# A Mamba and mixture-of-experts kernel: more of the scan's inputs turned on TensorE, and GpSimd given part of the elementwise work

## The chip, the cores and the metric

The kernel runs on one core of a Trainium2 chip. The metric is the time of one execution on the device in microseconds (us), the median of several runs. Five engines work side by side, each on its own instruction stream, in order: TensorE (PE; its weight loads are shown as PEld), VectorE (DVE), ScalarE (ACT), GpSimd (POOL) and SyncE (SP, which here only starts DMAs). They meet through semaphores.

## The reference

The input is x, 16 sequences of 256 time steps with 128 features. Three stages follow one another: half a mixture of experts (softmax over 8 experts, the top 2 of them, hidden size 512), a mixer, and the same mixture of experts again, each behind a layernorm and added to its input. In the mixer two Mamba blocks (with the same weights apart from the norm) follow one another, and a linear memory follows the second. What the change touches is the scan inside a Mamba block, with 256 channels d and 16 states s:

```python
def step(h, ins):
    d_t, B_t, C_t, u_t = ins
    dA = jnp.exp(d_t[:, :, None] * A)
    h = h * dA + (d_t * u_t)[:, :, None] * B_t[:, None, :]
    y = jnp.einsum('bds,bs->bd', h, C_t)
    return (h, y)
...
y = ys.transpose(1, 0, 2) + xm * D_ssm
y = y * jax.nn.silu(res)
```

## The kernel before

The 16 sequences form 8 groups of two. A group g passes four slots: slots 0 and 1 are the first Mamba block of its two sequences, slots 2 and 3 the second block. q = 4g + i counts slots, 32 in all. Beside the scans of its own slot every engine also does the preparation of the next slot (the head: norm, input projection, convolution, silu, x projection, softplus, du = delta * xm), the rest of the slot before (the tail: gate, output projection, memory), and pieces of the mixtures of experts of neighbouring groups. What each engine does in each of the four kinds of slot, and in which order, is written out by hand in `ORDER`. An engine never leaves that order.

A slot's 16 states are taken in 8 pairs j = 0 to 7. Tiles have 128 partitions; a pair is 2 states x 2 halves of the channels x 256 steps = 1,024 elements in each partition. For each pair:

- `d` (ScalarE, L973): dA = exp(A * delta), four instructions, into one of four buffers.
- The product du * B is made in one of two ways. In a direct pair (0, 2, 4, 6) TensorE spreads two rows of B over all partitions (`t`, L653; a matmul with a selector), and VectorE multiplies by du (`b`, L1331, into `dbu`). In a turned pair (1, 3, 5, 7) du already lies with time on the partitions (`duT`), so that B is a scalar of each partition: ScalarE multiplies with four instructions (`e`, L989, into `scaled`), and TensorE turns the result back into PSUM with eight transposes (`t`, L660).
- `s` (VectorE): the scan, either one of 1,024 elements from `dbu` (L1344) or two of 512 from PSUM (L1350).
- `k` (TensorE, L671) spreads the two rows of C, and `g` (VectorE, L1363) multiplies the states by them: pair 0 into `acc`, the others into one of three buffers `G`.
- `a` (GpSimd, L1602): a DMA that adds `G` to `acc` in memory. The seven of a slot follow one another, each waiting until the one before has landed.

`gate` (VectorE, L1371 to L1377) then waits for the last of them, adds the two states' halves of `acc`, adds D * xm and multiplies by silu(res).

The sorted mixtures of experts run beside this. VectorE finds each token's place (`fplace`, whose last result is `posi`, L1238), GpSimd scatters eight tiles of tokens with indirect DMAs (`sc0` to `sc7`, L1561), TensorE and ScalarE work through 15 tiles (`p`, and `F`, whose outputs L894 are sent out as `results`), GpSimd gathers eight tiles (`ga0` to `ga7`, L1573) once all of `results` have landed, and VectorE adds them up (`fsum`, L1255). Scatters of one mixture and gathers of another fall in slots 1 and 3, and `fsum` is VectorE's last step there; slots 0 and 2 have neither.

ScalarE needs one function table for exp (`d`, `sp`) and another for silu (`r`, `xm`, and the `F` pieces with a silu); each change of table is a load (L843).

## Time and profile before

| | |
|---|---|
| median of 3 runs | 1685.93 us (1684.01 to 1693.28) |
| the profiled execution, first to last instruction | 1689.5 us |
| VectorE busy | 1379.1 us (82%) |
| TensorE busy | 1330.0 us (79%) |
| ScalarE busy | 1278.8 us (76%) |
| GpSimd busy | 572.0 us (34%) |
| granted TensorE clock, mean | 0.90 |
| start up to the first slot's scans | about 87 us |
| from the last slot's end to the end | about 80 us |

Busy means that an instruction of that engine was under way. The profiled execution has only a span of its own, and no separate time on the device is given with it; its span lies 3.6 us above the median and inside the range of the three runs. The slots take some 1,490 us of it.

### The profile page before, as it was taken

How to read it: one execution, taken by the hardware profiler on the slowest of the kernel's cores; microseconds unless marked ns; L12 is line 12 of the kernel's file. 1: busy time of each engine (PE TensorE's matmuls, PEld its weight loads, DVE VectorE, ACT ScalarE, POOL GpSimd, SP SyncE). 2: the span in 40 equal slices, each digit the busy share in tenths (PEclk: the TensorE clock that was granted, in tenths of full speed). 3: DMA queues.
4: the chain of work that ended last, by engine and by line, in shares of the span. 5: the costliest groups of instructions: out<-in, count | busy, mean ns of one | idle time of the engine just before them, and what ended most of it. 6: DMA issues, size and time to landing. Idle time of an engine off the chain costs nothing. (4 is left out here: it accounts for less than half of the span.)

```text
span 1689.5 us, 29263 instructions
## 1 busy us (share of the span) xinstructions
PE 1330.0 (79%) x8754; PEld 1198.4 (71%) x8754; DVE 1379.1 (82%) x2183; ACT 1278.8 (76%) x2660; POOL 572.0 (34%) x617
## 2 busy tenths in 40 slices
PE   7978568878887787878878787887878787568778
PEld 6867457768777686767767676777867676457668
DVE  3367888989888888989889898989889888988732
ACT  3489657978789787978779698878789698549722
POOL 1211423162423426162423536163332523132210
PEclk9988668988999899998999799998999899778889
DMA  7346446675666767676666767675676765455731
GB/s 233 112 95 136 85 83 149 152 169 126 156 158 139 166 142 180 142 170 134 146 159 142 162 146 165 142 179 125 136 175 141 163 148 114 92 129 126 161 88 45
DMA packets 144662, 236.98 MB, mean 140 GB/s; under 512 B 13696, under 2 KB 79488, under 8 KB 144384
## 3 DMA queue, kind: packets, MB, share of 16 engines
q0 software_dynamic: 39424, 132.15, 40.7%
q1 hardware_dynamic: 105088, 102.97, 20.8%
q8 instruction: 77, 1.26, 0.3%
q14 instruction: 73, 0.60, 0.1%
HBM read 92.46 MB, written 25.17 MB: 70 GB/s over the span
## 5 line engine op out<-in xcount | busy, mean ns | idle before, releaser
L1602 POOL DMA_DIRECT2D acc<-G x224 | 204.2, 911 | 855.8 <-DMA acc<-G 422.1
L973 ACT ACTIVATE dA<-delta,A 128x255 f32<-128x255 f32 x1024 | 425.6, 495 | 6.3 <-DVE hs L1344 5.3
L1350 DVE TENSOR_TENSOR_SCAN hs<-dA,b_r 128x512 f32<-128x512 f32 x256 | 297.9, 1202 | 19.9 <-PE b_r L660 12.6
L1363 DVE TENSOR_TENSOR G<-hs,b_r 128x1024 f32<-128x1024 f32 x224 | 272.4, 1216 | 44.8 <-PE b_r L671 34.9
L1344 DVE TENSOR_TENSOR_SCAN hs<-dA,dbu 128x1024 f32<-128x1024 f32 x128 | 292.8, 2287 | 15.1 <-ACT dA L973 8.8
L535 PE MATMUL b_h<-xsT,wst 128*128 128x128 f32 x1680 | 255.5, 301 | 34.4 <-issue 23.3
L535 PEld LDWEIGHTS b_h<-xsT,wst 128*128 128x128 f32 x1680 | 230.5, 212 | 50.7 <-issue 49.0
L547 PE MATMUL b_out<-w2s,hT 128*128 x1680 | 239.0, 289 | 13.5 <-ACT ys L894 9.6
L843 ACT ACT_TABLE_LOAD x182 | 233.5, 1283 | 4.0 <-PEq L1733 0.7
L547 PEld LDWEIGHTS b_out<-w2s,hT 128*128 128x128 f32 x1680 | 219.9, 203 | 18.4 <-issue 17.0
L660 PE MATMUL b_r<-prm,scaled 128*128 128x128 f32 x1024 | 173.5, 300 | 59.7 <-ACT scaled L989 28.8
L989 ACT ACTIVATE scaled<-duT,dtT 128x256 f32<-128x256 f32 x512 | 217.0, 500 | 1.1 <-PE b_r L660 0.8
L660 PEld LDWEIGHTS b_r<-prm,scaled 128*128 128x128 f32 x1024 | 133.3, 156 | 76.5 <-DVE dbu L1331 33.4
L902 ACT ACTIVATE hT<-b_h 128x512 f32<-128x512 f32 x210 | 121.9, 595 | 84.6 <-PE b_h L535 83.5
L671 PE MATMUL b_r<-bcr,selr 128*128 128x256 f32 x512 | 136.0, 349 | 46.6 <-DVE G L1363 36.1
L1331 DVE TENSOR_TENSOR dbu<-du,b_r 128x1024 f32<-128x1024 f32 x128 | 155.3, 1213 | 6.1 <-PE b_r L653 5.8
L1561 POOL DMA_INDIRECT sorted<-xn,posi x112 | 134.7, 1203 | 63.4 <-DVE posi L1238 33.5
L1573 POOL DMA_INDIRECT yk<-results,posi x112 | 128.8, 1150 | 35.9 <-issue 34.2
L600 PE MATMUL b_w<-uT,inx 128*128 128x256 f32 x512 | 138.8, 408 | 1.2 <-ACT uT L918 0.7
L671 PEld LDWEIGHTS b_r<-bcr,selr 128*128 128x128 f32 x512 | 87.7, 207 | 64.3 <-DVE G L1363 45.2
L600 PEld LDWEIGHTS b_w<-uT,inx 128*128 128x128 f32 x512 | 94.4, 200 | 12.1 <-ACT uT L918 1.2
L653 PE MATMUL b_r<-bcr,selr 128*128 128x256 f32 x256 | 67.7, 350 | 42.5 <-DVE hs L1350 42.5
(176 smaller groups left out, 1974.3 us busy)
## 6 DMA issues: line engine op xcount, KB each, us to landing
acc<-G POOLq DMA_DIRECT2D x224, 512.0 KB, 4.8
wst<-w_dram SPq DMA_DIRECT2D x242, 256.0 KB, 2.9
xsort<-sorted SPq DMA_DIRECT2D x70, 192.0 KB, 5.2
results<-ys SPq DMA_DIRECT2D x70, 192.0 KB, 3.0
xin<-x_dram SPq DMA_DIRECT2D x8, 256.0 KB
sorted<-ys SPq DMA_DIRECT2D x2, 960.0 KB, 7.3
sorted<-xn,posi POOLq DMA_INDIRECT x112
yk<-results,posi POOLq DMA_INDIRECT x112
```

The source lines that it names most:

```text
L535: last = mm(H[r % 2][:, w], wst[k % NW][:, w], xsT[i // CH % 2][:, t:t + P], start=True, stop=True)
L547: last = mm(Y[:, i % CH * D:(i % CH + 1) * D], hT[i % NH][:, c, :], w2s[:, e, c, :], start=c == 0, stop=c == HC - 1)
L600: last = mm(o, inx[:, m, r, ch], uT[:, b, PAD - r:PAD - r + T], start=r == 0, stop=r == PAD)
L660: last = nc.tensor.transpose(R[u % 2][:, h * T + t * P:h * T + (t + 1) * P], scaled[k % 2][:, d, t, h * P:(h + 1) * P], ident)
L671: last = mm(C[:, d * T:(d + 1) * T], selr[:, SELECTED.index(DS + DP * j + d), :], bcr[b][:, :], start=True, stop=True)
L843: nc.scalar.preload_act_table_set(name)
L973: last = do(dA[j % 4][:, d, k, 1:], delta[b][:, k, 1:], ACT.Exp, scale=A[:, k, s:s + 1])
L989: last = do(scaled[n % 2][:, d, t, :], duT[b][:, t, :], ACT.Identity, scale=dtT[b][:, s:s + 1])
L1344: V.tensor_tensor_scan(flat(hs[j % 2]), flat(dA[j % 4]), flat(dbu[n % 2]), 0.0, ALU.mult, ALU.add)\
L1350: V.tensor_tensor_scan(hs[j % 2][:, d, :, :].rearrange("p h t -> p (h t)"), dA[j % 4][:, d, :, :].rearrange("p h t -> p (h t)"), R[u % 2][ ...
L1363: V.tensor_tensor(to[:, :, :, :], hs[j % 2][:, :, :, :], both(C).unsqueeze(2).broadcast_to([P, DP, HALVES, T]), ALU.mult).then_inc(q_G, 1)
L1602: Q.dma_start(acc[b][:, :, :, :].rearrange("p d h t -> p (d h t)"), G[j % NG][:, :, :, :].rearrange("p d h t -> p (d h t)"), accum_op=ALU. ...
```

## The change

Only pair 0 stays direct. Pairs 1 to 7 are all turned. Of these ScalarE makes 1, 3, 5 and 7 as before, and GpSimd makes 2, 4 and 6 (`e4`, `e6`, and `h2`, which makes pair 2 of the next slot ahead of it) with four multiplications of 128x256 each. `scaled` has four buffers in place of two. VectorE loses three of four `b` in a slot and has two scans of 512 in place of one of 1,024 in those pairs.

The sums now form two chains of DMAs: pair 0 and the even pairs in `acc`, pair 1 and the odd ones in a second tile, `odd`. Pair 1 is written there directly, and its DMA gives way to `skip`: GpSimd makes D * xm (two multiplications of 128x256) and a DMA adds it to `odd`. GpSimd then adds the halves of `acc` (`w1`), those of `odd`, and the two results (`w2`), three additions of 128x512. Of the four VectorE instructions in `gate` one is left, the product with silu(res).

The selectors are one column each, read 128 times with step zero, in place of full 128x128 tiles; they come with `prm`, so three loads of 512 KB and three casts in the start go. The order of all engines' work in the four kinds of slot is new.

```diff
-TURNED = (1, 3, 5, 7)
-DIRECT = tuple(j for j in range(NP) if j not in TURNED)
+DIRECT = (0,)
+TURNED = tuple(j for j in range(NP) if j not in DIRECT)
+POOLED = (2, 4, 6)
+NS = 4
+AHEAD = (2,)
 SELECTED = [DP * j + d for j in DIRECT for d in range(DP)] + list(range(DS, 2 * DS))
...
+def made_to(q, j):
+
+    by = POOLED if j in POOLED else [t for t in TURNED if t not in POOLED]
+    return q * len(by) + by.index(j) + 1
+
+
+EVEN = (2, 4, 6)
+ODD = ("skip", 3, 5, 7)
...
 ORDER = {
     "tensor": (
-        "p1 t0 k0 t1 in t2 p2 k1 t3 p1 t4 p1 k2 xp p1 t5 dt p1 t6 k3 p1 t7 m1 k4 t8 p1 dx p2 m2 k5 t9 p2 t10 m3 "
-        "t11 k6 p2 m4 k7 p1",
-        "t0 p1 t1 t2 p2 k0 p1 t3 p2 fturn k1 t4 t5 fgate p3 fcount p2 k2 p3 out t6 k3 p5 t7 turn t8 k4 in k5 t9 "
-        "k6 t10 xp t11 dt k7 dx",
-        "t0 p1 t1 p1 t2 p1 k0 t3 p3 k1 out p1 t4 p1 k2 t5 p1 t6 p1 turn t7 k3 in k4 t8 p1 xp t9 t10 dt k5 p1 t11 "
-        "p3 k6 p1 dx p2 k7",
-        "t0 t1 p3 t2 k0 p2 t3 p2 fturn p2 fgate k1 p1 t4 fcount t5 p2 turng k2 p1 in k3 t6 p4 k4 t7 t8 xp dt k5 "
-        "t9 t10 m1 t11 dx k6 m2 m3 k7 m4",
+        "p1 k0 p1 t0 t1 t2 p1 in t3 p2 t4 k1 xp t5 t6 p2 k2 dt p1 k3 t7 k4 t8 t9 p2 m1 dx t10 p1 k5 t11 t12 "
+        "m2 p2 k6 m3 p3 t13 t14 k7 m4 p2",
+        "t0 p1 t1 k0 p3 t2 t3 fturn p1 t4 fgate k1 p1 t5 t6 fcount k2 p5 k3 out t7 p3 k4 t8 t9 p3 turn k5 in "
+        "t10 t11 xp t12 k6 dt t13 dx k7 t14",
+        "p1 t0 p1 t1 p1 t2 p2 k0 t3 p1 k1 out t4 t5 k2 t6 p2 t7 p1 t8 turn p1 k3 in t9 p1 t10 k4 xp t11 t12 "
+        "dt k5 p3 k6 p1 t13 k7 p1 t14 dx p4",
+        "t0 k0 t1 t2 p2 fturn p3 fgate p1 k1 fcount t3 p1 t4 p1 turng p2 t5 p1 t6 p1 t7 t8 k2 in p1 k3 p2 k4 "
+        "xp dt t9 t10 t11 t12 k5 k6 m1 t13 t14 dx k7 m2 m3 m4",
     ),
     "scalar": (
-        "d0 e1 d1 d2 F0 e3 d3 F1 F2 e5 F3 r xm d4 proj d5 sp F4 F5 e7 F6 oT dx F7 d6 d7 v F8 rT",
-        "F9 e1 d0 d1 F10 F11 F12 e3 F13 d2 F14 F15 fxT d3 F16 F17 d4 F18 F19 d5 d6 F20 F21 e5 ftanh F22 F23 e7 "
-        "F24 turned r xm d7 proj sp dx",
-        "d0 e1 F0 d1 F1 F2 e3 F3 e5 F4 d2 d3 d4 d5 d6 turned d7 e7 F5 F6 r xm F7 proj F8 sp F9 F10 F11 dx",
-        "e1 F12 F13 d0 d1 F14 F15 e3 F16 F17 F18 fxT e5 F19 d2 d3 turned d4 F20 F21 ftanh F22 F23 r xm F24 d5 "
-        "proj e7 sp d6 oT dx v d7 rT",
+        "d0 e1 F0 d1 d2 d3 e3 F1 F2 e5 r xm F3 d4 proj e7 F4 F5 sp F6 d5 oT d6 dx d7 v F7 F8 F9 rT",
+        "e1 F10 F11 d0 F12 d1 F13 F14 d2 d3 fxT e3 d4 F15 F16 F17 F18 F19 e5 F20 ftanh d5 F21 d6 F22 F23 F24 "
+        "turned d7 e7 r xm proj sp dx",
+        "e1 d0 F0 d1 F1 d2 d3 F2 F3 e3 F4 d4 e5 d5 d6 turned d7 F5 e7 r xm F6 F7 F8 proj sp F9 F10 F11 dx",
+        "e1 F12 F13 d0 d1 F14 F15 e3 fxT F16 F17 F18 e5 d2 d3 F19 F20 turned F21 d4 d5 ftanh F22 e7 F23 r xm "
+        "F24 proj d6 sp oT d7 dx v rT",
     ),
     "vector": (
-        "b0 s0 g0 s1 gate g1 b2 s2 g2 s3 low b4 g3 delta s4 g4 s5 b6 mask g5 s6 g6 s7 xb g7",
-        "b0 fstats s0 s1 g0 fnorm b2 s2 flog ftop g1 fplace gate g2 s3 b4 xsum g3 un s4 g4 s5 g5 b6 fweights s6 "
-        "g6 low s7 delta g7 fsum",
-        "b0 s0 s1 g0 gate b2 g1 xsum s2 s3 un g2 b4 lx g3 s4 s5 g4 ln b6 low s6 g5 unx delta g6 s7 g7",
-        "b0 fstats s0 s1 fnorm b2 g0 flog ftop g1 fplace s2 g2 s3 gate g3 b4 s4 fweights g4 s5 low g5 b6 delta s6 "
-        "mask g6 s7 g7 xb fsum",
+        "b0 s0 s1 gate g0 s2 g1 s3 g2 low g3 s4 g4 delta s5 s6 mask g5 g6 s7 xb g7",
+        "fstats b0 s0 fnorm g0 s1 s2 flog ftop g1 fplace s3 g2 gate g3 xsum s4 un g4 s5 g5 s6 fweights low "
+        "delta g6 s7 g7 fsum",
+        "b0 s0 s1 g0 gate g1 s2 xsum s3 un g2 lx g3 s4 ln s5 g4 s6 g5 low unx g6 delta s7 g7",
+        "fstats b0 s0 fnorm g0 s1 flog ftop g1 fplace s2 s3 gate g2 s4 fweights g3 g4 s5 low g5 delta s6 g6 "
+        "s7 mask xb g7 fsum",
     ),
     "gpsimd": (
-        "a1 a2 a3 a4 a5 a6 a7",
-        "froot a1 sc0 sc1 sc2 a2 sc3 sc4 fkeep rms a3 sc5 sc6 sc7 rs a4 ga0 ga1 ga2 ga3 a5 ga4 ga5 ga6 ga7 a6 a7",
-        "a1 rms rs a2 a3 lnx rmsx a4 a5 a6 a7",
-        "froot a1 sc0 sc1 sc2 a2 sc3 sc4 fkeep a3 sc5 sc6 sc7 a4 ga0 ga1 ga2 ga3 a5 ga4 ga5 ga6 ga7 a6 a7",
+        "w1 w2 skip e4 e6 a2 a3 a4 a5 a6 h2 a7",
+        "froot e4 w1 w2 skip e6 sc0 sc1 a2 sc2 sc3 rms sc4 sc5 sc6 a3 a4 ga0 ga1 sc7 ga2 rs ga3 ga4 a5 ga5 "
+        "ga6 fkeep ga7 a6 a7 h2",
+        "e4 w1 w2 skip rms e6 a2 rs lnx a3 rmsx a4 a5 a6 h2 a7",
+        "w1 froot w2 skip e4 sc0 e6 sc1 sc2 sc3 a2 sc4 sc5 sc6 a3 sc7 a4 ga0 ga1 ga2 ga3 a5 ga4 ga5 ga6 ga7 "
+        "fkeep a6 a7 h2",
     ),
 }
...
-        selr = sb("selr", [P, len(SELECTED), P], fp32r)
+        selr = sb("selr", [P, len(SELECTED)], fp32r)
...
+        odd = [sb(f"odd{b}", [P, DP, HALVES, T]) for b in range(SEQ)]
+        xd = sb("xd", [P, HALVES, T])
...
-        scaled = [sb(f"scaled{i}", [P, DP, T // P, DI]) for i in range(2)]
-        dbu = [sb(f"dbu{i}", [P, DP, HALVES, T]) for i in range(2)]
+        scaled = [sb(f"scaled{i}", [P, DP, T // P, DI]) for i in range(NS)]
+        dbu = sb("dbu", [P, DP, HALVES, T])
...
+        def scaled_free(q, j):
+
+            k = TURNED.index(j)
+            before = [(p, t) for p in (q - 1, q) for t in TURNED][:len(TURNED) + k]
+            p, t = [x for x in before if x[1] % NS == j % NS][-1]
+            return p * NU + UNIT_OF["S", DP * t + DP - 1] + 1
+
+        def landed(q, j):
+
+            if j in EVEN:
+                return q_even, 16 * (q * len(EVEN) + EVEN.index(j) + 1)
+            return q_odd, 16 * (q * len(ODD) + ODD.index(j) + 1)
...
+            def selector(row):
+                k = SELECTED.index(row)
+                return selr[:, k:k + 1].broadcast_to([P, P])
...
-                was, m = UNITS[u - 2]
-                p = q if u >= 2 else q - 1
+                all_units = q * NU + u
+                p, w = divmod(all_units - 2, NU)
+                was, m = UNITS[w]
+                into = R[all_units % 2]
                 if was == "B":
-                    wait(pe, q_dbu, p * len(DIRECT) + DIRECT.index(m) + 1)
+                    wait(pe, q_dbu, p + 1)
                 else:
                     wait(pe, q_scan, scans_to(p, m // DP) - (DP - 1 - m % DP))
                 if kind == "B":
-                    if n == DIRECT[0]:
-                        pe.wait_ge(q_bc, q + 1)
+                    pe.wait_ge(q_bc, q + 1)
                     for d in range(DP):
-                        last = mm(R[u % 2][:, d * T:(d + 1) * T], selr[:, SELECTED.index(DP * n + d), :], bcr[b][:, :],
+                        last = mm(into[:, d * T:(d + 1) * T], selector(DP * n + d), bcr[b][:, :],
                                   start=True, stop=True)
                 else:
-                    k, d = TURNED.index(n // DP), n % DP
-                    pe.wait_ge(q_sc, q * len(TURNED) + k + 1)
+                    j, d = n // DP, n % DP
+                    pe.wait_ge(q_made if j in POOLED else q_sc, made_to(q, j))
                     for h in range(HALVES):
                         for t in range(T // P):
-                            last = nc.tensor.transpose(R[u % 2][:, h * T + t * P:h * T + (t + 1) * P],
-                                                       scaled[k % 2][:, d, t, h * P:(h + 1) * P], ident)
+                            last = nc.tensor.transpose(into[:, h * T + t * P:h * T + (t + 1) * P],
+                                                       scaled[j % NS][:, d, t, h * P:(h + 1) * P], ident)
                 last.then_inc(q_B, 1)
...
             def du_turned(g, i):
                 q, b = 4 * g + i, i % 2
                 act.wait_ge(q_dumm, q + 1)
+                wait(act, q_made, (q - 1) * len(POOLED))
                 do(duT[b][:, :, :], W[1][:, :].rearrange("p (j d) -> p j d", d=DI), ACT.Copy).then_inc(q_duT, 1)
 
             def scale(g, i, j):
-                q, b, n = 4 * g + i, i % 2, TURNED.index(j)
+                q, b = 4 * g + i, i % 2
                 act.wait_ge(q_duT, q + 1)
-                p, k = (q, n - 2) if n >= 2 else (q - 1, n - 2 + len(TURNED))
-                wait(act, q_B, p * NU + UNIT_OF["S", DP * TURNED[k] + 1] + 1)
+                wait(act, q_B, scaled_free(q, j))
                 for d in range(DP):
                     for t in range(T // P):
                         s = T + t * DS + DP * j + d
-                        last = do(scaled[n % 2][:, d, t, :], duT[b][:, t, :], ACT.Identity, scale=dtT[b][:, s:s + 1])
+                        last = do(scaled[j % NS][:, d, t, :], duT[b][:, t, :], ACT.Identity,
+                                  scale=dtT[b][:, s:s + 1])
                 last.then_inc(q_sc, 1)
...
-                if j:
-                    last = j - NG if j > NG else max(p for p in range(1, NP) if p % NG == j % NG) - (NP - 1)
-                    wait(dve, q_gs, (q * (NP - 1) + last) * 16)
-                to = G[j % NG] if j else acc[i % 2]
+                if j >= 2:
+                    wait(dve, *(landed(q, j - NG) if j - NG >= 2 else landed(q - 1, j - NG + NP - 2)))
+                to = G[(j - 2) % NG] if j >= 2 else (acc, odd)[j][i % 2]
                 V.tensor_tensor(to[:, :, :, :], hs[j % 2][:, :, :, :],
                                 both(C).unsqueeze(2).broadcast_to([P, DP, HALVES, T]), ALU.mult).then_inc(q_G, 1)
 
             def gate_y(g, i):
                 q, b = 4 * g + i, i % 2
-                dve.wait_ge(q_gs, (q + 1) * (NP - 1) * 16)
+                dve.wait_ge(q_sum, 3 * q + 3)
                 dve.wait_ge(q_res, 2 * q + 2)
                 wait(dve, q_omm, q)
-                V.tensor_tensor(yg[:, :, :], acc[b][:, 0, :, :], acc[b][:, 1, :, :], ALU.add)
-                dve.drain()
-                for k in range(HALVES):
-                    V.scalar_tensor_tensor(out=yg[:, k, :], in0=xm[b][:, k, :], scalar=par("D_ssm")[:, k:k + 1],
-                                           in1=yg[:, k, :], op0=ALU.mult, op1=ALU.add)
-                dve.drain()
-                V.tensor_tensor(yg[:, :, :], yg[:, :, :], sres[b][:, :, :], ALU.mult).then_inc(q_yg, 1)
+                V.tensor_tensor(yg[:, :, :], acc[b][:, 0, :, :], sres[b][:, :, :], ALU.mult).then_inc(q_yg, 1)
...
-                wait(pool, q_gs, (q * (NP - 1) + j - 1) * 16)
-                Q.dma_start(acc[b][:, :, :, :].rearrange("p d h t -> p (d h t)"),
-                            G[j % NG][:, :, :, :].rearrange("p d h t -> p (d h t)"),
-                            accum_op=ALU.add).then_inc(q_gs, 16)
+                if j in EVEN:
+                    wait(pool, *(landed(q, j - 2) if j > 2 else landed(q - 1, 6)))
+                    Q.dma_start(flat(acc[b]), flat(G[(j - 2) % NG]), accum_op=ALU.add).then_inc(q_even, 16)
+                else:
+                    pool.wait_ge(*landed(q, j - 2 if j > 3 else "skip"))
+                    Q.dma_start(flat(odd[b]), flat(G[(j - 2) % NG]), accum_op=ALU.add).then_inc(q_odd, 16)
+
+            def skip(g, i):
+
+                q, b = 4 * g + i, i % 2
+                pool.wait_ge(q_xm, 2 * q + 2)
+                for k in range(HALVES):
+                    Q.tensor_scalar(xd[:, k, :], xm[b][:, k, :], par("D_ssm")[:, k:k + 1], 1.0,
+                                    ALU.mult, ALU.mult).then_inc(p_skip, 1)
+                pool.wait_ge(q_G, q * NP + 2)
+                wait(pool, *landed(q - 1, 7))
+                pool.wait_ge(p_skip, 2 * q + 2)
+                Q.dma_start(odd[b][:, 0, :, :], xd[:, :, :], accum_op=ALU.add).then_inc(q_odd, 16)
+
+            def merge(g, i, k):
+
+                q, b = 4 * g + i, i % 2
+                if k == 1:
+                    pool.wait_ge(*landed(q, 6))
+                    Q.tensor_tensor(acc[b][:, 0, :, :], acc[b][:, 0, :, :], acc[b][:, 1, :, :], ALU.add)\
+                        .then_inc(q_sum, 1)
+                else:
+                    pool.wait_ge(*landed(q, 7))
+                    Q.tensor_tensor(odd[b][:, 0, :, :], odd[b][:, 0, :, :], odd[b][:, 1, :, :], ALU.add)\
+                        .then_inc(q_sum, 1)
+                    pool.wait_ge(q_sum, 3 * q + 2)
+                    Q.tensor_tensor(acc[b][:, 0, :, :], acc[b][:, 0, :, :], odd[b][:, 0, :, :], ALU.add)\
+                        .then_inc(q_sum, 1)
+
+            def scale(g, i, j):
+                q, b = 4 * g + i, i % 2
+                pool.wait_ge(q_dt, q + 1)
+                pool.wait_ge(q_duT, q + 1)
+                wait(pool, q_B, scaled_free(q, j))
+                for d in range(DP):
+                    for t in range(T // P):
+                        s = T + t * DS + DP * j + d
+                        last = Q.tensor_scalar(scaled[j % NS][:, d, t, :], duT[b][:, t, :], dtT[b][:, s:s + 1], 1.0,
+                                               ALU.mult, ALU.mult)
+                last.then_inc(q_made, 1)
...
+                for j in AHEAD:
+                    scale(0, 0, j)
...
+                merge(GROUPS - 1, 3, 1)
                 ffn_root(LAST, one)
+                merge(GROUPS - 1, 3, 2)
```

## Rows read from the trace of the kernel before

**Rows 1.** Windows: us, PE, PEld, DVE, ACT, POOL busy (instructions), clock, DMA share, GB/s.
```profile
85.00:1576.00 1491.00, 1167.10 (x7713) 1048.81 (x7711) 1298.22 (x1920) 1204.20 (x2521) 539.60 (x569) 0.89 0.64 142
...
672.00:712.90 40.90, 34.47 (x240) 30.91 (x237) 39.93 (x43) 37.50 (x76) 5.19 (x6) 0.92 0.64 138
712.90:767.40 54.50, 41.09 (x276) 37.30 (x274) 45.63 (x84) 41.59 (x85) 30.13 (x30) 0.87 0.74 168
767.40:813.80 46.40, 39.67 (x281) 37.16 (x282) 43.98 (x70) 41.58 (x86) 14.50 (x19) 0.93 0.66 146
813.80:863.00 49.20, 40.85 (x276) 36.57 (x276) 39.90 (x70) 38.70 (x87) 26.57 (x24) 0.97 0.67 156
```

**Rows 2.** Waits of VectorE, 85 to 1576 us: us in total, times, longest.
```profile
DVE ob L1255 <- DMA yk<-results,posi: 18.5, 6, 4.0
...
DVE xa L1255 <- DMA yk<-results,posi: 14.9, 7, 3.1
```

**Rows 3.** Timeline of VectorE, one second slot: start us, us, operation.
```profile
899.84 1.22 DVE L1331 TENSOR_TENSOR dbu<-du,b_r 128x1024 f32<-128x1024 f32 x1
...
919.71 0.17 DVE L1238 CAST posi<-posf 128x8 uint32<-128x8 f32 x1
...
940.55 2.29 DVE L1344 TENSOR_TENSOR_SCAN hs<-dA,dbu 128x1024 f32<-128x1024 f32 x1
...
952.64 2.35 DVE L1255 SCALAR_TENSOR_TENSOR xa<-yk,c,xa 128x128 f32<-128x128 f32 x8 [3.10 <-DMA yk<-results,posi]
```

**Rows 4.** Timeline of GpSimd, the same slot.
```profile
940.65 2.95 POOL L1573 DMA_INDIRECT yk<-results,posi  x1 [0.31 <-issue]
...
950.12 0.95 POOL L1573 DMA_INDIRECT yk<-results,posi  x1 [0.30 <-issue]
```

**Rows 5.** Groups of VectorE by line: busy us, mean ns of one, idle before.
```profile
L1350 DVE TENSOR_TENSOR_SCAN hs<-dA,b_r 128x512 f32<-128x512 f32 x256 | 297.9, 1202 | 19.9 <-PE b_r L660 12.6 <-ACT dA L973 7.1
...
L1344 DVE TENSOR_TENSOR_SCAN hs<-dA,dbu 128x1024 f32<-128x1024 f32 x128 | 292.8, 2287 | 15.1 <-ACT dA L973 8.8
...
L1331 DVE TENSOR_TENSOR dbu<-du,b_r 128x1024 f32<-128x1024 f32 x128 | 155.3, 1213 | 6.1 <-PE b_r L653 5.8
...
L1374 DVE SCALAR_TENSOR_TENSOR yg<-xm,prm,yg 128x256 f32<-128x256 f32 x64 | 28.2, 482 | 2.5
...
L1371 DVE TENSOR_TENSOR yg<-acc 128x512 f32<-128x512 f32 x32 | 21.9, 683 | 2.7 <-DMA acc<-G 2.5 <-issue 0.2
```

**Rows 6.** Groups of ScalarE and TensorE by line, the same columns.
```profile
L843 ACT ACT_TABLE_LOAD x182 | 233.5, 1283 | 4.0 <-PEq L1733 0.7
...
L660 PE MATMUL b_r<-prm,scaled 128*128 128x128 f32 x1024 | 173.5, 300 | 59.7 <-ACT scaled L989 28.8 <-DVE dbu L1331 24.5 <-DVE hs L1350 6.2
...
L653 PE MATMUL b_r<-bcr,selr 128*128 128x256 f32 x256 | 67.7, 350 | 42.5 <-DVE hs L1350 42.5
```

**Rows 7.** Groups of GpSimd by line, shapes kept apart, the same columns.
```profile
L1561 POOL DMA_INDIRECT sorted<-xn,posi x112 | 134.7, 1203 | 63.4 <-DVE posi L1238 33.5 <-issue 29.0 <-DMA acc<-G 0.9
...
L1573 POOL DMA_INDIRECT yk<-results,posi x112 | 128.8, 1150 | 35.9 <-issue 34.2 <-DMA results<-ys 1.6
...
L1611 POOL TENSOR_TENSOR rs<-xam,x 128x256 f32<-128x256 f32 x16 | 14.6, 910 | 0.2
...
L1579 POOL TENSOR_SCALAR xam<-xa 128x256 f32<-128x256 f32 x2 | 0.8, 400 | 0.0
```

**Rows 8.** One line's instructions: ns min/median/max, first and last start.
```profile
L1561 POOL DMA_INDIRECT sorted<-xn,posi x112: 954/982/2863, 53.5 to 1507.0; - x112
...
L1573 POOL DMA_INDIRECT yk<-results,posi x112: 940/992/2952, 172.8 to 1608.7; - x112
```

**Rows 9.** DMA issues on the page: KB each, median us to landing.
```profile
acc<-G POOLq DMA_DIRECT2D x224, 512.0 KB, 4.8
...
results<-ys SPq DMA_DIRECT2D x70, 192.0 KB, 3.0
```

**Rows 10.** Timeline of ScalarE, the same slot: the last results copied out.
```profile
931.83 0.47 ACT L894 ACTIVATE ys<-b_out 128x384 f32<-128x384 f32 x1
```

74 lines of the change are left out of this document (39 added, 35 removed).

## The prediction

> **What bounds the kernel now.** I read the windows of each kind of slot first. Over all slots VectorE is busy 1,298 of 1,491 us, ScalarE 1,204, TensorE 1,167, GpSimd 540 [rows 1]. The four windows below that row are slots 0 to 3 of one group, cut at each slot's first `g`. In slot 0 VectorE works 39.9 of 40.9 us and in slot 2 44.0 of 46.4: there it is the bound. In slots 1 and 3 it works 45.6 of 54.5 and 39.9 of 49.2, and something else sets the length [rows 1].
>
> VectorE's waits say what: `fsum` waits 18.5 + 14.9 us for gathers, thirteen times [rows 2]. The timelines of one slot 1 show the chain. The slot starts at 899.84, the places are written at 919.88, the last gather's issue ends at 951.07, `fsum` starts at 952.64 after a wait of 3.10 and ends at 954.99 [rows 3, 4]. So 55.2 us = 20.0 (VectorE up to the places) + 31.2 (GpSimd) + 1.6 (landing) + 2.4 (`fsum`). GpSimd's 31.2 us are one unbroken queue by the written order: eight scatters, eight gathers, four accumulating DMAs and three small steps. A GpSimd busy only a third of the time is the bound of half the slots.
>
> **VectorE, removed.** Three `b` at 155.3/128 = 1.21 us each are 3.64 us a slot. A pair turned instead of direct costs two scans of 297.9/256 = 1.16 against one of 292.8/128 = 2.29: 0.04 more, 0.12 a slot. The gate loses one addition (0.68) and two instructions of 28.2/64 = 0.44: 1.57 [rows 5]; their drains I count at nothing. Sum: 3.64 - 0.12 + 1.57 = 5.1 us a slot, 163 us in 32. That is the most the change can give through VectorE. The selectors' casts lie beside a start in which TensorE runs without gaps: nothing.
>
> **TensorE.** 24 more transposes at 173.5/1024 = 0.17 are 4.1 us a slot, six fewer matmuls at 67.7/256 = 0.26 are 1.6 [rows 6]: 2.5 us more. In slot 2 that makes 39.7 + 2.5 = 42.2 of 46.4, part of it at a clock below full (0.93) [rows 1]. It hides behind ScalarE; without that cover it costs up to 2.5 us a slot. The selector weights read with step zero have no row. Between no change and a doubling of their share of the load, 18 loads a slot at the order of 0.1 us, lies 0 to 2 us, hidden too; I take 0.
>
> **ScalarE.** It makes as many products as before. But if I follow the new order through the slots and count where exp and silu alternate, there are 30 more table loads than the 182: two more in each slot 2 and slot 3 that has pieces. 30 x 1.283 = 38.5 us [rows 6]. ScalarE is busy 37.5 of 40.9 in slot 0 and 41.6 of 46.4 in slot 2 [rows 1]; with two loads the latter becomes 44.2. So in slots 0 and 2 it is next in line right behind VectorE. VectorE offers 5.1, ScalarE lets some 2.4 and 2.2 through. It runs up to four pairs ahead and can lend work to slots 1 and 3, where it has room: I take 2.5 for each.
>
> **GpSimd, added.** The multiplication with a column of scalars is in no row. The nearest is the multiplication by a constant on 128x256 at 400 ns [rows 7]. Lower end: that. Upper end: the addition with two tensor inputs of the same size, 910 ns [rows 7]. A column adds one element to each partition's reads, so I take 400: 14 of them are 5.6 us. For the additions of 128x512 there are 910 ns for half the size and twice that; I take 1.3: 3.9 us. Together 9.5 us a slot, 7 to 18 by the ends. The number of DMAs stays at seven.
>
> By the Trainium skill (GPSIMD Engine Reference, Performance versus the Vector engine) an addition of two fp32 tensors costs about 2.6 cycles an element and one-input work runs about at line rate; as an estimate from that page three additions would be 3.3 us instead of 3.9. Its section on engine selection speaks against moving such work to GpSimd at all.
>
> Where does it lie? `e4`, `w1`, `w2`, `skip` and in slot 1 `e6` come ahead of the first scatter, in time that GpSimd now waits away. In slot 3 `e6` (1.6) is inside the chain and `fkeep` has gone out of it. In slots 1 and 3 `h2` comes after the last gather. In slots 0 and 2 the queue has room (5.2 of 40.9 and 14.5 of 46.4 busy [rows 1]). So it is nearly hidden as long as the multiplications cost what I think.
>
> **The new waits.** `w2` waits for pair 7's DMA (4.8 us [rows 9]), and then two additions stand between it and the gate, where VectorE's drop in: 2.6 us later than before. In slots 0 and 2, which follow on late gathers, the gate at 6 to 7 us into the slot is close to that; queued behind it is all of VectorE. I take 0, because ScalarE bounds those slots; the upper end is 3 us. `skip` waits for pair 1's `g`; behind it are `e4` or `e6` and the scatters, and the placing on VectorE takes about as long as they do.
>
> **The gather chain.** Two things shorten it. First, one `b` less ahead of the places: 1.2 us. Second, a gather that started at 940.65, inside a VectorE scan with two inputs in SBUF (940.55, 2.29 us), took 2.95 us [rows 3, 4]; the median is 0.99 [rows 8]. Mean less median over both kinds is (1.203 - 0.982 + 1.150 - 0.992) x 112 = 42 us, 3.0 for each of 14 slots [rows 7, 8]. After the change only pair 0's scan reads `dbu`, ahead of the scatters. I take 2.
>
> The Trainium skill (SBUF — State Buffer, Who interferes with whom) says that a VectorE instruction with two SBUF inputs and a GpSimd instruction that reads SBUF exclude each other for the whole instruction. The trace agrees: 2.95 against 0.99 us.
>
> One thing holds it back: the gathers need the last `results`. They are copied out at 931.83 [rows 10] and land 3.0 us after their issue [rows 9], near 936; gathering began soon after. In slot 3's new order `F24` comes after 32 us of ScalarE's own work where it came after 26 (my count with its durations). There the first gather will wait for it. I take 3 us for slot 1 and 2 for slot 3.
>
> **Sum.** A group gains 2.5 + 3 + 2.5 + 2 = 10 us. Groups 1 to 6: 60. In groups 0 and 7 four slots have little or no expert work, and there VectorE's relief comes through nearly whole, 4 us each, and 2.5 in the other four: 26. The end: the last DMAs no longer form one chain ahead of GpSimd's root: 2. Together 88. 1689.5 - 88 = 1601.5, and as the profiled span stood 3.6 above the median, 1598.
>
> **Rivals.**
> - *VectorE's relief lands whole.* If ScalarE can shift its work and the gather chain shrinks by 5 a slot: 1689.5 - 163 - 3.6 = 1523. For it: ScalarE waits much in slots 1 and 3. Against: 31 us of GpSimd queue.
> - *ScalarE and the chain hold.* The first gather waits for `results` in both slots, the gate for `w2`: slots 1 and 3 stay at 55, groups gain 5: 30 + 18 + 2 = 50, 1636. For it: gathering began only some 2 us after the results; 30 more table loads.
> - *Slower: the multiplication by a column is dear.* If one costs c us, slot 3 has eight of them around the chain and slot 1 four that its slack of some 1 us doesn't hold: a group loses 12(c - 0.4) - 2. From c = 1.4 the gain of 10 is gone; at c = 2 a group is 7 us longer, 6 x 7 = 42, 1728. For it: no such row, and 910 ns with two inputs. Against: 400 ns [rows 7].
> - *No change: the two engines block each other.* GpSimd has 17 more instructions that read SBUF in each slot. If each held VectorE up for 0.3 us, 5.1 are gone, 1680. For it: 2.95 against 0.99, seen from the other side. Against: what VectorE runs is mostly scans and `g` with one input in PSUM; rows 8's medians show that those leave GpSimd alone.
>
> **Numbers.** Forecast 0.50, relief whole 0.14, chain holds 0.20, dear multiplication 0.09, blocking 0.07. About 0.5% (8 us) is what a measurement of this kernel can tell from no change. So faster 0.84, same 0.07, slower 0.09. The likeliest case alone spans 1565 to 1630. The range takes in half of the full relief and most of the chain case, 1545 to 1665, and leaves out about 2 in 10.
>
> **What would show it.** VectorE busy near 1,216 in all; ScalarE near 1,317; 212 table loads; GpSimd near 875. Slots 0 and 2 near 38 and 42 with ScalarE full; slots 1 and 3 near 52, `fsum` still waiting for gathers; indirect DMAs at means near 1.0; multiplications on GpSimd at 0.4. It is wrong if these cost 1 us or more, if VectorE waits at the gate for `w2`, or if the gathers wait for `results` longer than the scatter queue's own length.

## The result, and the profile of the changed kernel

The changed kernel takes 1820.1 us (median of 4 runs, 1808.0 to 1824.4), the kernel before 1685.0 beside it (4 runs). The ratio is 1.078, 95% interval 1.074 to 1.082: slower by 7.8%. The forecast was 1598 us, range 1545 to 1665. Profiled: a span of 1806.2 us against 1689.5.

The head of the page of the changed kernel: busy time, share of the span, instructions of each engine.

```profile
span 1806.2 us, 31047 instructions
...
PE 1422.3 (79%) x9330; PEld 1275.1 (71%) x9330; DVE 1311.7 (73%) x2085; ACT 1327.7 (74%) x2690; POOL 896.1 (50%) x1161
```

VectorE is busy 67 us less than before (1379.1), where 163 us were to go. ScalarE (forecast 1317) and GpSimd (forecast 875) came out near the forecast.

The cuts of [rows 1] at each slot's first `g` don't compare the two kernels: the new order moves a scan and the gate past that `g`. So I cut at pair 0's product `dbu`, the first VectorE work of a slot in both. Slots 0 to 3 of one group, first the kernel before, then the changed one, columns as in [rows 1]:

```profile
859.30:899.80 40.50, 32.12 (x217) 28.77 (x218) 36.86 (x34) 32.90 (x67) 5.16 (x6) 0.92 0.63 140
899.80:954.90 55.10, 40.98 (x291) 36.20 (x290) 46.81 (x92) 44.69 (x91) 29.94 (x30) 0.92 0.73 166
954.90:999.10 44.20, 38.16 (x241) 35.60 (x242) 40.70 (x57) 36.16 (x75) 12.50 (x16) 0.82 0.57 121
999.10:1054.80 55.70, 44.98 (x322) 40.34 (x321) 45.36 (x85) 46.39 (x104) 28.83 (x27) 1.00 0.73 168
```
```profile
923.10:965.00 41.90, 37.62 (x268) 34.71 (x269) 33.90 (x40) 35.55 (x73) 16.90 (x23) 0.92 0.56 125
965.00:1025.70 60.70, 46.35 (x303) 41.91 (x301) 44.00 (x81) 45.19 (x88) 39.37 (x49) 0.86 0.59 141
1025.70:1067.30 41.60, 36.59 (x258) 32.46 (x257) 38.98 (x62) 38.12 (x77) 22.70 (x34) 0.96 0.59 130
1067.30:1130.80 63.50, 46.62 (x316) 41.27 (x315) 46.07 (x74) 47.32 (x101) 37.94 (x44) 0.92 0.59 143
```

Slots 0 and 2 together stayed within 2 us (84.7 and 83.5 here, 81.2 and 83.0 in the mean of groups 1 to 5 below); slots 1 and 3, which carry the scatters and gathers, grew from 55 to 61 and 64 us. VectorE does 44.0 and 46.1 us of work in them, hardly less than before, although three products and most of the gate have gone. Its groups by line say why; the columns are those of [rows 5].

```profile
L1378 DVE TENSOR_TENSOR_SCAN hs<-dA,b_r 128x512 f32<-128x512 f32 x448 | 526.6, 1207 | 185.2 <-PE b_r L691 154.5 <-issue 19.5 <-ACT dA L1005 9.1
...
L1372 DVE TENSOR_TENSOR_SCAN hs<-dA,dbu 128x1024 f32<-128x1024 f32 x32 | 87.7, 2741 | 4.2
...
L1285 DVE SCALAR_TENSOR_TENSOR ob<-yk,c,ob 128x128 f32<-128x128 f32 x56 | 37.8, 734 | 0.5
L1285 DVE SCALAR_TENSOR_TENSOR xa<-yk,c,xa 128x128 f32<-128x128 f32 x56 | 36.1, 704 | 0.7
...
L1185 DVE TENSOR_SCALAR xn<-xin,mv,rstd 128x128 f32<-128x128 f32 x32 | 19.7, 679 | 3.1 <-POOL rstd L1561 3.1
L1185 DVE TENSOR_SCALAR xn<-xb,mv,rstd 128x128 f32<-128x128 f32 x32 | 13.9, 496 | 1.1 <-POOL rstd L1561 1.1
```

The same groups in the kernel before, `fsum` and `xn`:

```profile
L1255 DVE SCALAR_TENSOR_TENSOR xa<-yk,c,xa 128x128 f32<-128x128 f32 x56 | 16.0, 348 | 15.4 <-DMA yk<-results,posi 14.9
...
L1155 DVE TENSOR_SCALAR xn<-xin,mv,rstd 128x128 f32<-128x128 f32 x32 | 8.9, 343 | 7.2 <-POOL rstd L1540 7.2
```

The scan whose second input lies in PSUM costs what it did, 1207 ns against 1202 [rows 5]. The scan with both inputs in SBUF went from 2287 to 2741 ns. `fsum` (L1285; it writes `xa` in slots 1 and `ob` in slots 3) took 348 ns an instruction before in both kinds of slot, and `xn` 343 and 346. The same lines compared over all of VectorE, mean times count, cost some 80 us more: 42 in `fsum`, 15.6 in `xn`, 14.5 in pair 0's scan, the rest small. The first row shows the other change: scans wait 154.5 us for TensorE's turns, against 12.6 [rows 5].

One of the two longest of the fourteen `fsum`s and what GpSimd does beside it, from the two timelines of the changed kernel (VectorE, then GpSimd):

```profile
1229.46 9.81 DVE L1285 SCALAR_TENSOR_TENSOR xa<-yk,c,xa 128x128 f32<-128x128 f32 x8
1239.19 1.21 DVE L1360 TENSOR_TENSOR dbu<-du,b_r 128x1024 f32<-128x1024 f32 x1
```
```profile
1230.46 3.90 POOL L1667 TENSOR_SCALAR scaled<-duT,dtT 128x256 f32<-128x256 f32 x8
1234.25 1.34 POOL L1649 TENSOR_TENSOR acc<-acc 128x512 f32<-128x512 f32 x1
1235.48 1.33 POOL L1653 TENSOR_TENSOR odd<-odd 128x512 f32<-128x512 f32 x1
1236.89 1.26 POOL L1656 TENSOR_TENSOR acc<-acc,odd 128x512 f32<-128x512 f32 x1
1238.14 1.00 POOL L1637 TENSOR_SCALAR xd<-xm,prm 128x256 f32<-128x256 f32 x2
```

Eight instructions that take 2.35 us alone [rows 3] take 9.81, and end 0.1 us after GpSimd's unbroken series of products (`h2` and the next slot's `e4`) and the next slot's sums. GpSimd runs at its own pace meanwhile. One of the eight, 6168 ns long, stands still while most of the products and two additions go by. That `dbu`, with one input in PSUM, costs 1.21 as ever.

Not every `fsum` fares like this. In eight of the fourteen one instruction stands still, for 3.2 us in six of them and for 6.2 us in two. In five the eight instructions take 3.4 us, none over 0.67 us, while GpSimd's products keep their pace of 0.48 us from start to start; the two engines then seem to take turns. The hold-up falls on the next slot's scan instead, which took 5.0 to 5.1 us in four of these five and 3.8 us in the fifth:

```profile
818.16 3.40 DVE L1285 SCALAR_TENSOR_TENSOR xa<-yk,c,xa 128x128 f32<-128x128 f32 x8
821.48 1.21 DVE L1360 TENSOR_TENSOR dbu<-du,b_r 128x1024 f32<-128x1024 f32 x1
822.82 5.00 DVE L1372 TENSOR_TENSOR_SCAN hs<-dA,dbu 128x1024 f32<-128x1024 f32 x1
```

GpSimd's groups in the changed kernel, the columns of [rows 7]:

```profile
L1667 POOL TENSOR_SCALAR scaled<-duT,dtT 128x256 f32<-128x256 f32 x384 | 209.7, 721 | 14.6 <-issue 14.2
L1582 POOL DMA_INDIRECT sorted<-xn,posi x112 | 113.8, 1016 | 46.3 <-issue 28.4 <-DVE posi L1268 17.9
L1594 POOL DMA_INDIRECT yk<-results,posi x112 | 113.1, 1010 | 91.7 <-DMA results<-ys 62.8 <-issue 28.6 <-DMA odd<-G 0.3
...
L1656 POOL TENSOR_TENSOR acc<-acc,odd 128x512 f32<-128x512 f32 x32 | 54.0, 1686 | 2.5
```

The product with a column costs 0.55 us busy, 0.48 from start to start in the series above (its mean of 721 ns counts overlap); scatters and gathers are no longer held up (1203 and 1150 before [rows 7]); but the first gather waits 62.8 us for results, against 1.6. The DMA list of the page has their landing at 4.9 us, against 3.0 [rows 9]:

```profile
results<-ys SPq DMA_DIRECT2D x70, 192.0 KB, 4.9
```

The two medians don't compare like with like: the trace of the changed kernel has the landing of only 42 of the 70 transfers, and in `fsum_clear` below, with all 70, the median is 3.1 us although the first gather waits as long (64.2 us in all). What did grow is the landing of the last results of a slot 1: 3.8 us in the mean of groups 1 to 5 before, 6.0 after.

To see where in a slot the time goes I took milestones from the timelines: us from the slot's `dbu` of pair 0, mean of groups 1 to 5; the last `ys` and the last gather by their ends, the first gather by its start (`all_write_only`, an experiment below, is the changed kernel without GpSimd's new reads).

```
                     slot 1                          slot 3
                 before  changed  all_write_only  before  changed  all_write_only
last ys copied    33.4    34.3      31.1           31.9    34.9      32.1
first gather      38.5    41.3      38.0           38.8    39.7      37.0
last gather       51.3    55.0      51.8           51.3    50.9      48.3
fsum starts       52.9    57.3      54.3           53.2    56.6      53.5
fsum ends         55.3    63.3      56.6           55.5    62.3      55.9
next slot         55.2    63.2      56.5           55.5    62.2      56.3
slots 0 and 2:    before 38.6, 42.6   changed 41.3, 41.7   all_write_only 39.5, 41.0
```

The end of `fsum` is the end of the slot in every column. Of the 14.7 us that slots 1 and 3 grew by, 7.0 are `fsum` itself (2.4 to 6.0 us in slot 1, 2.3 to 5.7 in slot 3), the rest its later start.

### The profile page after: what moved, and what is told of

The parts are those of the page before. It is cut to its first block and busy times, and to the rows that moved or that the text cites. A ratio compares the mean times of both kernels' runs of the same rounds, so it can differ in the third digit from the quotient of the medians.

```text
span 1806.2 us, 31047 instructions
## 1 busy us (share of the span) xinstructions
PE 1422.3 (79%) x9330; PEld 1275.1 (71%) x9330; DVE 1311.7 (73%) x2085; ACT 1327.7 (74%) x2690; POOL 896.1 (50%) x1161
## 5 line engine op out<-in xcount | busy, mean ns | idle before, releaser
L1378 DVE TENSOR_TENSOR_SCAN hs<-dA,b_r 128x512 f32<-128x512 f32 x448 | 526.6, 1207 | 185.2 <-PE b_r L691 154.5
L691 PE MATMUL b_r<-prm,scaled 128*128 128x128 f32 x1792 | 304.3, 304 | 120.3 <-DVE hs L1378 56.8
L691 PEld LDWEIGHTS b_r<-prm,scaled 128*128 128x128 f32 x1792 | 234.1, 157 | 161.6 <-DVE hs L1378 79.7
L874 ACT ACT_TABLE_LOAD x212 | 272.0, 1283 | 4.5 <-PEq L1812 0.7
L1390 DVE TENSOR_TENSOR G<-hs,b_r 128x1024 f32<-128x1024 f32 x192 | 233.2, 1214 | 49.1 <-PE b_r L702 41.7
L1667 POOL TENSOR_SCALAR scaled<-duT,dtT 128x256 f32<-128x256 f32 x384 | 209.7, 721 | 14.6 <-issue 14.2
L702 PE MATMUL b_r<-bcr,selr 128*128 128x256 f32 x512 | 135.7, 349 | 63.7 <-DVE G L1390 59.9
L1630 POOL DMA_DIRECT2D odd<-G x96 | 88.0, 917 | 181.9 <-DVE G L1390 177.0
L1627 POOL DMA_DIRECT2D acc<-G x96 | 90.5, 943 | 157.3 <-DVE G L1390 116.8
L1594 POOL DMA_INDIRECT yk<-results,posi x112 | 113.1, 1010 | 91.7 <-DMA results<-ys 62.8
L702 PEld LDWEIGHTS b_r<-bcr,selr 128*128 128x128 f32 x512 | 86.2, 209 | 80.3 <-DVE G L1390 60.0
L1582 POOL DMA_INDIRECT sorted<-xn,posi x112 | 113.8, 1016 | 46.3 <-issue 28.4
L1642 POOL DMA_DIRECT2D odd<-xd x32 | 29.0, 907 | 198.1 <-DVE odd L1390 130.7
```

Source lines behind the costliest of these rows:

```text
L691: last = nc.tensor.transpose(into[:, h * T + t * P:h * T + (t + 1) * P], scaled[j % NS][:, d, t, h * P:(h + 1) * P], ident)
L702: last = mm(C[:, d * T:(d + 1) * T], selector(DS + DP * j + d), bcr[b][:, :], start=True, stop=True)
L874: nc.scalar.preload_act_table_set(name)
L1378: V.tensor_tensor_scan(hs[j % 2][:, d, :, :].rearrange("p h t -> p (h t)"), dA[j % 4][:, d, :, :].rearrange("p h t -> p (h t)"), R[u % 2][ ...
L1390: V.tensor_tensor(to[:, :, :, :], hs[j % 2][:, :, :, :], both(C).unsqueeze(2).broadcast_to([P, DP, HALVES, T]), ALU.mult).then_inc(q_G, 1)
L1667: last = Q.tensor_scalar(scaled[j % NS][:, d, t, :], duT[b][:, t, :], dtT[b][:, s:s + 1], 1.0, ALU.mult, ALU.mult)
```

## The experiments

All ratios are to the kernel before, run beside each version on the same chip. Its medians there lie between 1684.8 and 1689.6 us, so differences of times taken beside different ones carry up to 5 us. Two theories at the start: **the lock**, GpSimd instructions that read SBUF hold up VectorE instructions with their operands in SBUF; and **the queue**, every scan's input now waits for its turn on TensorE, which has two banks for them.

**1. Reads of GpSimd taken away.** Three kernels write what they would compute.

```
-  Q.tensor_scalar(scaled[...], duT[...], dtT[...], 1.0, mult, mult)      # mult_write_only
+  Q.memset(scaled[...], 0.01)
-  Q.tensor_tensor(acc[b][:, 0], acc[b][:, 0], acc[b][:, 1], ALU.add)     # adds_write_only: the 3 additions
+  Q.memset(acc[b][:, 0], 0.01)                                           # all_write_only: both, and xd
```

> The changed kernel with GpSimd's twelve multiplications of a slot turned into memsets of the same tiles: they write but read nothing, so the products of pairs 2, 4 and 6 are left out of the result. Theory of the lock (GpSimd's reads hold up VectorE's instructions with two inputs in SBUF; the same lines cost VectorE 81 us more than before): fsum's instructions fall from 720 to about 350 ns, pair 0's scan from 2741 to 2290, and the time falls by 50 to 80 us, to 1740 to 1770. Theory of the queue (VectorE waits 154 us for turned units behind other work on TensorE, and the slots 1 and 3 follow a chain of preparation): those durations fall, but the waits grow instead, and the time stays within 20 us of 1820.

> As the one before, and also the three additions and the two multiplications by D of each slot as memsets, so the sums are left out as well: none of the change's work on GpSimd reads SBUF, its DMAs and waits all stay. Lock: another 10 to 20 us less than the kernel with only the multiplications as memsets. Queue: no further change beyond 5 us. If this kernel still stands above 1685, the lock and GpSimd's added time together are not the whole of the loss, and the rest lies in the turned pairs and the order.

> The changed kernel with GpSimd's three additions a slot replaced by writes of the same tiles (the sums over pairs are left out); its twelve products with a column stay. Taking the products' reads away as well brought 1714.6 us from 1782.3. The theory of the lock, with the two kinds of work independent: 1820 - 68 = 1752 us, 1740 to 1765, fsum still near 700 ns (the products stand beside it), scan0 near 2400 and xn near 346 ns. The rival (the additions matter only as time in GpSimd's queue ahead of the products): 1800 us or more, since a write takes nearly as long as an addition.

Measured: `mult_write_only` 1782.3 us (1.054, 1.049 to 1.059), `adds_write_only` 1745.5 (1.034, 1.029 to 1.039), `all_write_only` 1714.6 (1.017, 1.013 to 1.020). Against 1820 taking away the products is worth 38 us, the additions 75, all together 105: nearly the sum. The first is less than the 50 to 80 us expected, and the last gained 68 us over the first where 10 to 20 were expected. In `all_write_only` VectorE's lines are back:

```profile
L1372 DVE TENSOR_TENSOR_SCAN hs<-dA,dbu 128x1024 f32<-128x1024 f32 x32 | 73.4, 2292 | 4.2
...
L1285 DVE SCALAR_TENSOR_TENSOR ob<-yk,c,ob 128x128 f32<-128x128 f32 x56 | 16.0, 346 | 0.6
```

`xn` isn't quite back in this run (460 and 365 ns).

VectorE's busy time fell by 24, 45 and 81 us, in the order of the results. But GpSimd's queue got shorter as well, and its busy time fell by 95, 87 and 210 us. The products' writes in `mult_write_only`:

```profile
L1667 POOL MEMSET scaled<- 128x256 f32 x384 | 117.5, 538 | 13.7 <-issue 13.7
```

That is 0.31 us busy for a write where the product has 0.55; the mean of 538 ns counts overlap. The additions' writes take 0.53 to 0.69 us for 1.4 to 1.7. So these three runs show what GpSimd's new work costs with its reads, 105 of the 135 us, and can't tell the hold-up of VectorE from the longer queue. Experiment 2 can. Some 30 us over the kernel before stay, with 149 us less VectorE work. Two windows of `all_write_only`, a slot 0 and a slot 2, cut at `dbu`, show who ends them now:

```profile
681.20:720.30 39.10, 35.78 (x271) 32.85 (x271) 33.39 (x39) 36.58 (x76) 10.72 (x23) 0.99 0.61 137
...
776.60:817.70 41.10, 36.00 (x261) 31.80 (x260) 37.09 (x62) 38.90 (x78) 16.81 (x35) 0.99 0.63 138
```

VectorE has room (33.4 of 39.1, 37.1 of 41.1), ScalarE has little (36.6 and 38.9) and TensorE not much more. The slots 0 take 39.5 us in the mean where they took 38.6: the relief isn't seen there, and it isn't in slots 1 and 3, whose ends are `fsum`'s (table above).

**2. One instruction series moved.** The same program, but `h2` waits for `fsum` in slots 1 and 3.

```
-  "... a5 ga5 ga6 fkeep ga7 a6 a7 h2"
+  "... a5 ga5 ga6 fkeep ga7 a6 a7 y h2"      # y: pool.wait_ge(f_yacc, f[0])
```

> The changed kernel; in slots 1 and 3 GpSimd's product h2 waits until VectorE's sum over the two experts (fsum) is done. Nothing else moves. The theory of the lock on a tied path: fsum back from 5.6 us to under 3 us in 14 slots, 35 to 45 us, less what h2 and the additions behind it (now 2 us later) cost the next scan and the gate: 1780 to 1800 us. The rival (the delay of h2 and of the sums costs as much): 1810 to 1835.

Measured: 1763.2 us (1.048, 1.041 to 1.055). `fsum` is back at 346 ns:

```profile
L1285 DVE SCALAR_TENSOR_TENSOR ob<-yk,c,ob 128x128 f32<-128x128 f32 x56 | 16.0, 346 | 2.0 <-DMA yk<-results,posi 1.4
```

Every computation is there, and GpSimd is as busy as in the changed kernel (904 us against 896). VectorE lost 50 us of busy time and the kernel 57 us: this settles that the hold-up lies on the path, and that one placement cost 57 of the 135 us. How the other 48 of experiment 1's 105 us divide between hold-up and queue no run separates. The gate now waits 26.0 us for the additions (2.9 before), a small price. The gain was larger than I expected (1780 to 1800); pair 0's scan, which gained too (2741 to 2393 ns), is 11 us of it.

**3. The parts of the change apart.** `sums_only` has the sums and the one-column selectors on the kernel before; `pairs_only` has everything but the sums; `old_order` is the changed program with TensorE, ScalarE and VectorE in the order of the kernel before (GpSimd's order stays the new one).

```
sums_only   gpsimd slot 1   -  "froot a1 sc0 ..."   +  "froot w1 w2 skip sc0 ..."
pairs_only  gpsimd slot 1   -  "froot e4 w1 w2 skip e6 sc0 ..."   +  "froot e4 a1 e6 sc0 ..."
old_order   tensor slot 1   "t0 p1 t1 t2 p2 k0 p1 t3 t4 p2 fturn k1 t5 t6 fgate ..."   # each old b unit: two turns
```

> The kernel before with only the change's sums (two chains of DMAs, skip, GpSimd's three additions, one instruction left in the gate) and its one-column selectors; pairs, products and the order of TensorE, ScalarE and VectorE are the old ones. Queue: the loss comes with the turned pairs, so this is no slower than before, and 10 to 40 us faster: 1645 to 1680. Lock: GpSimd's five new reading instructions meet four scans a slot with two inputs in SBUF, so it gains little or nothing, 1675 to 1720.

> The changed kernel without its sums: one chain of transfers, VectorE's gate of four instructions, no addition and no product with D on GpSimd. The turned pairs, GpSimd's twelve products and the new order stay. If the parts add up (the sums alone cost nothing), 1805 to 1830 us. The theory of the lock: GpSimd's additions cost 68 us in the changed kernel (the difference of the two write-only runs), the work given back to VectorE is 32 x (683 + 2 x 482) ns = 53 us, so 1785 to 1815 with scan0 near 2450 ns and xn near 346 ns. Under 1750 would mean that sums and pairs hurt only together.

> The changed kernel in the order of the kernel before on TensorE, ScalarE and VectorE: each old unit that made a pair's product over two rows becomes the two turned units, in the same place; the three products that VectorE made drop out; two places where that would wait in a circle are put the other way round; GpSimd's order stays as in the change. If the new order is what costs the time: 1700 to 1760 us. If the turned pairs are, because no scan has its input before TensorE comes to it in its queue: 1800 to 1850 us, with VectorE's waits for TensorE's turns at 100 us or more either way.

Measured: 1686.2 us (0.999, 0.997 to 1.001), 1859.7 (1.100, 1.094 to 1.105) and 1922.9 (1.139, 1.133 to 1.145). The sums alone cost nothing and win 40 us beside the turned pairs. The new order is worth 103 us to them: it isn't the culprit. The turned pairs lose in either order. `pairs_only` came out above the 1785 to 1830 us that I gave it, and it loses most of its time without the lock: its `fsum` takes 372 and 363 ns, pair 0's scan 2346, and over all of VectorE the stretching is some 17 us. With one chain of sums GpSimd stands 423 us behind its own DMAs, and VectorE's `xn` waits for GpSimd's root, 62.3 us in all against 4.2 in the changed kernel:

```profile
POOL acc L1633 <- DMA acc<-G: 423.0, 115, 7.5
...
DVE xn L1185 <- POOL rstd L1568: 62.3, 14, 7.7
```

The single chain cost the kernel before about as much waiting on GpSimd (422.1 us) but only 15.4 us at `xn`. So there is a second way in which the turned pairs lose, through the start of a slot, which the two chains of the change relieve. Only these waits show it; no run tested it. In `old_order` VectorE's `g` waits 142.5 us for TensorE's spread, beside 74.5 at the scans; my expected 1800 to 1850 for the queue was too little.

**4. The lock in the sums alone.** In `sums_only` the additions stood beside `xn` (756 and 668 ns). `sums_late` holds them back until `xn` is made.

```
-  "froot w1 w2 skip sc0 ..."
+  "froot n w1 w2 skip sc0 ..."      # n: pool.wait_ge(f_xn, fx[0] + 1), slots 1 and 3
```

> The kernel before with the sums of the change alone (two chains of transfers, the product with D and three additions by GpSimd, the one-instruction gate), and GpSimd's additions at the start of slots 1 and 3 held back until VectorE has made xn. In sums_only xn cost 756 and 668 ns where the kernel before has 343 and 346, 24 us in all, and its other VectorE work fell by 46 us. The theory of the lock (a GpSimd instruction that reads SBUF holds up a VectorE instruction with its operands in SBUF, and those 24 us lie on the path): xn back at 345 ns, and 1655 to 1672 us, a ratio of 0.980 to 0.990. The rival (VectorE isn't what the sums would have to relieve, the chains are): xn back at 345 ns, and 1680 to 1692 us all the same.

Measured: 1667.5 us (0.988, 0.984 to 0.991), 1.2% faster than the kernel before. `xn` is back:

```profile
L1164 DVE TENSOR_SCALAR xn<-xb,mv,rstd 128x128 f32<-128x128 f32 x32 | 9.0, 340 | 2.0 <-POOL rstd L1542 2.0
L1164 DVE TENSOR_SCALAR xn<-xin,mv,rstd 128x128 f32<-128x128 f32 x32 | 8.8, 337 | 0.0
```

One wait, 24 us of VectorE time in `xn` (17 us of its busy time in all, since some small instructions now meet the additions instead), 19 us of the kernel. Of the versions run it is the fastest.

**5. The theory of the queue.** `turns_first` puts two turns ahead of the input projection in slot 1, and a third ahead of the x projection (its expectation has that one unmoved); `pair4_direct` gives pair 4 back to VectorE; `no_downs_two` leaves out TensorE's down products and ScalarE's waits for them, and `no_downs_three` gives their bank to the turns.

```
turns_first     -  "turn k5 in t10 t11 xp t12"      +  "turn k5 t10 t11 in t12 xp"
pair4_direct    -  DIRECT = (0,)                     +  DIRECT = (0, 4)
no_downs_three  -  into = R[all_units % 2]           +  into = R[all_units % 3]      # R[2] = the bank b_out
```

> The changed kernel with one move in TensorE's order of slot 1: the transposes t10 and t11 go ahead of the input projection, and t12 ahead of the x projection stays where it was. In the trace the second scan of pair 5 waits 6.0 us there, for transposes that stand behind 5 us of the projection's matmuls. Queue: the wait of 6 us goes in each of eight slots 1, and 15 to 45 us of the time with it. Lock: less than 10 us. If the chain of preparation sets the slot, not the scans, the wait moves to delta or the gathers and nothing is gained.

> The changed kernel with pair 4 made as before the change: TensorE spreads two rows, VectorE multiplies, one scan of 1024 columns; GpSimd makes two pairs in place of three. VectorE has 32 products of 1213 ns more, 39 us. The theory of the queue (a turned unit's input can be made only when the scan two units back is through, so every stop of TensorE for the preparation stops the scans; a product by VectorE frees the bank early and leaves a scan of 2.3 us in hand): VectorE's waits for TensorE's turns fall from 154.5 us to under 110, and 1740 to 1795 us in spite of the added work. The rival (the cost lies in GpSimd's instructions and what they hold up): its products go from 12 to 8 a slot, which is worth a third of the 38 us that mult_write_only brought, so with the 39 us added 1825 to 1850.

> The changed kernel without the mixtures' down products on TensorE (15 x 4 matmuls each of 14 times, left out; ScalarE copies a constant of the same size into ys, so the rest of the mixtures' work and transfers stands). It is the yardstick for no_downs_three, and tells by itself what TensorE's own work in the queue costs. The theory of the queue: scans wait behind those products too, 1680 to 1760 us. The rival (the scans wait for the preparation's chain alone, or for GpSimd): 1780 to 1820.

> no_downs_two with the bank that the down products leave free given to the scans' inputs: three banks in turn in place of two, so that TensorE can be three units ahead of VectorE's scans. If the two banks are what ties the scans to TensorE's queue: 40 to 100 us under no_downs_two, VectorE's waits for TensorE's turns less than half. If not (the order in the queue alone, or the chain from gate to delta, sets it): within 10 us of no_downs_two, the waits moved to TensorE's next stop.

Measured: 1815.4 us (1.076, 1.072 to 1.080), 1843.0 (1.091, 1.087 to 1.095), 1794.4 (1.064, 1.059 to 1.069) and 1801.5 (1.068, 1.061 to 1.075). None of the four bears the theory out. `turns_first` cut the waits for turns from 154.5 to 122.1 us and gained nothing that can be told from noise. Another product for VectorE did not pay. Taking 132 us of work from TensorE gained 26. Part of that may be hidden: with less work TensorE had a lower granted clock, 0.850 in `no_downs_two` and 0.830 in `no_downs_three` against 0.889, so these two runs aren't clean tests. The third bank gained nothing, and the waits stayed (139.6 and 29.7 us here, 144.8 in `no_downs_two`):

```profile
DVE hs L1374 <- PE b_r L689: 139.6, 48, 7.3
...
DVE hs L1374 <- PE b_out L689: 29.7, 37, 2.4
```

The 154.5 us of VectorE's waits for turns are the largest idle time on the page of the changed kernel, and no run that shortened them alone gained by it: they look like slack, in which VectorE waits there instead of later.

**6. The two ends that meet at fsum.** Slots 1 and 3 end with `fsum`. `fsum` stands behind VectorE's own order and behind results, landing, gathers. `pairs_ahead` shortens the first; `no_gathers` takes the second away as well; `gate_early` moves the gate of slot 1 to its start and rewrites the slot after it.

```
pairs_ahead   vector slot 1   -  "g5 s6 fweights low delta g6 s7 g7 fsum"   +  "g5 s6 g6 s7 g7 fweights low delta fsum"
no_gathers    -  Q.indirect_dma_start(yk[:, k, j, :], None, ys_d[m % 2], ...)   +  return
gate_early    vector slot 1   -  "s0 fnorm g0 s1 s2 flog ... s3 g2 gate g3"     +  "s0 fnorm g0 s1 gate s2 flog ..."
gate_early_slot3, turned_best   vector slot 3   -  "xb g7 fsum"      +  "g7 fsum xb"
sums_best                       vector slot 3   -  "g7 xb fsum"      +  "g7 fsum xb"
```

> The changed kernel with another order in slot 1 alone: TensorE turns t10 to t14 and spreads k6, k7 ahead of dt and dx, and VectorE scans pair 7 and makes g6, g7 ahead of fweights, low and delta. The theory of the chain (a slot is as long as the way to the gate, the chain gate to du of 28 us, and the VectorE work that stands behind du; VectorE idles between gate and delta, so work put there is free): 6 us less behind du, 4 to 6 us less in each of 8 slots 1, 1770 to 1795 us. The rival (the turned units' queue): the same work in front of dt stops TensorE at t13, t14 and k7, dt comes later by as much, and 1805 to 1840.

> pairs_ahead (1800 us) without the mixtures' gathers: the 8 indirect transfers of a pass from the results are left out, fsum reads a constant and waits for none. VectorE waited 36.6 us for them there. The theory of two tied ends (fsum stands behind both VectorE's own work and the chain last results, landing, eight gathers): with one end gone the slot falls back on the other, 1740 to 1770 us. If the gathers bound alone: under 1730. If they don't bind: 1785 or more.

> The changed kernel with slot 1 written anew around an early gate: VectorE does the gate right after s1 (the sums are ready 4 us after the slot's start, the changed kernel's gate stands at 16 to 18), TensorE's out follows t2, GpSimd makes the root ahead of skip, and turn, in, xp, dt, dx follow about 9 us earlier on all engines. The theory of the chain: du 8 to 10 us earlier, the slot shorter by 4 to 9 us until VectorE's own 47 us of work set it: 1750 to 1790. The rival (the work ahead of the old gate, routing and its waits, only moves behind it): du earlier by under 4 us, 1800 to 1830.

> gate_early, and in slot 3 two moves: xb, which waited 30 us in all for the end of the memory chain on TensorE, goes behind fsum, and GpSimd's additions wait until xn is made. The theory of the chain and of the lock: 3 us a slot 3 from xb and 1 to 2 from xn, 25 to 40 us below gate_early. If xb's wait is only moved to the next slot's first instructions that need it: within 10 us of gate_early.

Measured: `pairs_ahead` 1800.1 us (1.068, 1.062 to 1.075), `no_gathers` 1776.9 (1.053, 1.048 to 1.059), `gate_early` 2030.7 (1.206, 1.198 to 1.214), `gate_early_slot3` 1971.4 (1.167, 1.159 to 1.176). With its own work out of the way VectorE waited for the gathers instead:

```profile
DVE xa L1275 <- DMA yk<-results,posi: 36.6, 7, 7.5
```

and without gathers the kernel gained 23 us more. In slot 1 `fsum` then starts at 50.0 us instead of 56.1 and the slot takes 52.4 us instead of 63.2, but slot 2 grows from 40.4 to 46.9 us with ScalarE busy 44.7 us of them (34.8 in `pairs_ahead`): a large part of what slot 1 gives is taken back by ScalarE's work in the next slot. So both ends lie some 6 us apart in slot 1, and a third, ScalarE, stands close behind. Both gains fell short of what I gave (1770 to 1795 and 1740 to 1770 us). `gate_early` did get the gate of slot 1 at 9.8 us after `dbu` in place of 22.9; `un` came only 3.5 us earlier, the first gather at 72.8 us instead of 41.3, and the slot grew to 95 us. It is one step moved by hand in a web of four written orders: it tests my order, not the chain. The two moves in slot 3 were worth 59 us on top of it; in `turned_best`, too, `fsum` starts 51.4 us into slot 3 where the changed kernel has 56.6, and no longer stands behind `xb`, which waits 30.0 us in all for TensorE's memory chain in the changed kernel.

**7. Best versions.**

> The changed kernel with what the runs so far point to: slot 1 as in pairs_ahead, h2 behind fsum in slots 1 and 3, in slot 3 xb behind fsum and the additions behind xn. From 1800 (pairs_ahead): fsum 40 us, slot 3 30 to 45 us (gate_early_slot3 gained 59 us over gate_early by these two moves), so 1705 to 1740, still no better than the kernel before. If fsum's end was tied to the gathers in slot 3 as well: 1750 or more.

> sums_late (1667 us) with xb behind fsum in slot 3. There xb waited 9.8 us in all for TensorE's memory chain and fsum 15 us for gathers. The theory of two tied ends: up to 8 us less, 1655 to 1665. If fsum waits the same time for the gathers instead: 1662 to 1672.

Measured: `turned_best` (experiment 2's wait, `pairs_ahead`'s order, additions behind `xn` and `xb` behind `fsum` in slot 3) 1734.0 us (1.027, 1.021 to 1.033); `sums_best` 1684.3 (0.999, 0.997 to 1.001), 17 us behind `sums_late`: moving `xb` took back what the `xn` wait had brought. The move bought no earlier `fsum` (51.0 us into slot 3 in `sums_late`, 51.4 in `sums_best`), and slot 0 grew from 37.6 to 39.8 us. Why was not followed up. The turned pairs were not made to pay in any version.

## Why the prediction was wrong

**Right.** The reading of what bounds which slot. The counts and own costs: 212 table loads (x212, 272.0 us), ScalarE 1328 against 1317, the product with a column at 0.5 us, not 1.4 or more (so that rival, though slower like the result, is not what happened), the additions at 1.3 us where nothing crosses them, gathers and scatters 37 us shorter against 42. The selectors read with step zero cost nothing: their weight loads take 209 ns (L702) where full tiles took 207 (L671). GpSimd's 896 against 875 is partly luck: its new work measured 12.2 us a slot where 9.5 were counted, and the shorter gathers and scatters and some smaller differences made up for it. (By its own terms the lower end of "7 to 18" is 8.3 us.) The gate waited 2.9 us for `w2`, taken as 0. VectorE's relief is real: without GpSimd's reads it is busy 1230 us against the forecast 1216.

**The step that failed first** is GpSimd's "so it is nearly hidden as long as the multiplications cost what I think". It priced GpSimd's new work by its own time alone, and placed it where GpSimd was free. The slot order shows what that place was: `h2` "after the last gather" is exactly beside `fsum`, `w1 w2 skip` beside `xn` or pair 0's scan. The forecast used the lock in one direction (VectorE's scans slow a gather, [rows 3, 4]) and counted its end as a gain; the other direction was priced at nothing. Measured: some 80 us of VectorE time; 57 us of the kernel by one placement alone (experiment 2), and 105 us for all of GpSimd's reads together with its longer queue (experiment 1). The sentence from the Trainium skill that the prediction cited (SBUF — State Buffer, Who interferes with whom) excludes both ways; the timelines above agree, 9.81 us for 2.35, and show what it doesn't say, that one VectorE instruction can stay behind several of GpSimd's in a row.

**The rival that named it**, "the two engines block each other", was right in mechanism and had 0.07. Its argument against, that VectorE mostly runs instructions with an input in PSUM, is true (1207 ns stayed 1207), and beside the point: the few with both inputs in SBUF stand at the end and the start of a slot, where GpSimd's series was put. It also gave 1680 as the time, because it took the whole relief of 163 us as its gain; that gain was not there to be cancelled.

**The second failed step** is the sum's "2.5 + 3 + 2.5 + 2", 10 us gained a group. Without the lock a group takes 193.4 us where it took 191.9. Slots 0 and 2 gained 0.7 us together instead of 5: ScalarE, which the prediction put "next in line right behind VectorE", is busy 37.8 of 39.5 us in slots 0 and 38.8 of 41.0 in slots 2 (33.6 of 38.6 and 37.1 of 42.6 in the kernel before; means of groups 1 to 5). It did not "lend work to slots 1 and 3": its 5.2 us more a group all lie in slots 0 and 2. Slots 1 and 3 lost 2.1 us instead of gaining 5. In slot 1 the last results are copied out 2.3 us earlier, but the first gather starts 6.9 us after them instead of 5.1 (their landing takes 6.0 us, before 3.8), and the series of gathers takes 13.8 us instead of 12.8. In slot 3 the gathers are done 3.0 us earlier, as forecast, and `fsum` starts 0.3 us later all the same, behind VectorE's own order with `xb`. So the terms "3 for slot 1 and 2 for slot 3" were right about the gathers of slot 3 alone, and treated the end of the gathers as the end of the slot. The rival "ScalarE and the chain hold" described this best; it expected 5 us gained a group, and there are -1.5.

**What stays open.** Of the 20 us by which the profiled span of `all_write_only` is longer than that of the kernel before, 7 lie ahead of the first slot's `dbu` (at 93.5 us in place of 86.8), 11 in groups 0 to 6 and 8 in group 7; 6 come back after the last `g`. The longer start comes with the new order: `old_order` has that `dbu` at 86.8, `pairs_only` at 92.9. Why the last results of a slot 1 land later is not shown. The two chains of DMAs alone don't do it: in `sums_only`, which has them, the first gather of a slot 1 starts 4.3 us after the last results are copied out, against 5.1 before. The new order is ruled out as the cause of the loss; a third bank and the down products brought little or nothing, at a lower clock.

## What to carry to other kernels

Before moving work to GpSimd, write beside each moved instruction which VectorE instruction will run at that moment and where its operands lie: if both read SBUF the VectorE instruction can stand still while several GpSimd instructions go by, and one semaphore wait that moves the series away from it can be worth 3% (57 us here) or turn a neutral change into a gain (1686 to 1667). The longest wait on the page need not be the bound: of 154.5 us of waits for turns a fifth could be removed, and it bought nothing. Work taken off the busiest engine pays only in slots which that engine ends; trace where the next slot's start comes from in each kind of slot before multiplying a saving by the number of slots.

## What the runs showed of the hardware that was not expected

A VectorE instruction of 345 ns (128x128, all operands in SBUF) was stretched to 6.2 us by GpSimd instructions one after another; GpSimd's own kept their pace, 0.48 us each from start to start in the same series. `TENSOR_SCALAR` with one tensor input in SBUF suffers too (`xn`, 343 to 679 ns). GpSimd writes without reads (memset) beside the same `fsum` did not stretch it (346 ns in `all_write_only`). `xn` they did: in that run the 22 of its 64 instructions that lay beside a memset of `acc` took 548 to 559 ns in the mean, the 36 with nothing of GpSimd beside them 338.

TensorE's clock: these windows of the changed kernel, 4 us each in one slot 1, show it at its lower level (0.50, that is 1.2 GHz) after TensorE stood almost still for 4 us while it waited for `du`. It stays there through the next three windows, in which the engine is 59 to 91% busy, and into the fourth. In the first window it was low for a while too (0.65), with the engine busy throughout.

```profile
804.40:808.40 4.00, 4.00 (x18) 3.37 (x16) 1.78 (x4) 2.20 (x4) 3.36 (x4) 0.65 0.17 50
808.40:812.40 4.00, 0.15 (x2) 0.00 (x0) 1.98 (x4) 2.58 (x6) 3.25 (x4) 0.78 0.74 193
812.40:816.40 4.00, 3.64 (x15) 3.13 (x15) 3.36 (x4) 2.59 (x6) 3.50 (x4) 0.50 1.07 256
816.40:820.40 4.00, 2.37 (x11) 2.21 (x11) 3.77 (x8) 3.98 (x10) 3.26 (x6) 0.50 0.69 144
820.40:824.40 4.00, 3.00 (x13) 2.22 (x12) 3.87 (x5) 3.96 (x7) 4.00 (x9) 0.50 0.97 208
824.40:828.40 4.00, 3.56 (x18) 3.35 (x16) 4.00 (x2) 3.97 (x9) 3.92 (x3) 0.59 0.18 33
828.40:832.40 4.00, 2.87 (x19) 2.27 (x20) 4.00 (x5) 3.12 (x7) 1.41 (x3) 1.00 0.10 39
```

Four transposes take 1.12 us there and 0.60 at full clock. In the windows of the result slot 1 has a mean granted clock of 0.86 where it had 0.92, and in the run without GpSimd's reads the whole kernel's is 0.913 against 0.889. That may be part of what each us of hold-up cost; it is not shown apart.
